# Row maxima of the first query block taken inside the projections, which load its keys block by block, last tokens first

## What is computed

```python
# layer 0, causal
q = (x @ W_q) ; lat = x @ W_dkv
lat = (lat - mean) * rsqrt(var + 1e-5) * ln_gamma + ln_beta
k = lat @ W_uk ; v = lat @ W_uv
q = apply_rope(q) ; k = apply_rope(k)
scores = einsum('bhqd,bhkd->bhqk', q, k) / sqrt(16)      # masked above the diagonal
out = einsum('bhqk,bhkd->bhqd', softmax(scores), v) @ W_o
# layer 1, not causal: Q, K, V from x by wq, wk, wv; rope on Q and K; softmax(Q K / 4) V
```

## Time and profile before

| what | value |
|---|---|
| median of 3 runs | 5580.25 us (5573.52 to 5586.86) |
| the profiled execution | 5566.02 us, its span 5564.2 us |
| mean granted clock of TensorE | 0.936 |
| busy: TensorE, VectorE, ScalarE, POOL | 91%, 85%, 67%, 4% |
| projections of layer 0, then of layer 1 | 2 to 195 us, 2345 to 2472 us |

### The profile page before, as it was taken

The page is one execution under the profiler, slowest core; times in us unless marked ns, Lnnn a source line. Parts: engine busy times, 40 slices in busy tenths (PEclk is TensorE's granted clock), DMA queues, the critical chain, the costliest instruction groups (busy, mean ns, idle before and its releaser), DMA issues. The chain is left out here.

```text
span 5564.2 us, 124831 instructions
## 1 busy us (share of the span) xinstructions
PE 5047.7 (91%) x43370; PEld 2092.7 (38%) x43370; DVE 4709.1 (85%) x5375; ACT 3734.5 (67%) x7102; POOL 218.6 (4%) x278
## 2 busy tenths in 40 slices
PE   7599999999999588767999999999999999999686
PEld 4233434433444255432333333333333333333332
DVE  3588889889888689739999999999999999999535
ACT  2068787787777311123888888888888888888331
POOL 3100000000000000030000000000000000000201
PEclk7589999999999799986999999999999999999886
DMA  4301010010010100060100001000100001000000
GB/s 125 102 18 31 14 35 15 11 41 8 11 41 11 27 11 12 17 204 12 41 8 5 5 18 31 5 5 8 38 8 8 5 5 41 8 5 5 8 0 30
DMA packets 152926, 142.93 MB, mean 26 GB/s; under 512 B 72490, under 2 KB 107242, under 8 KB 152298
## 3 DMA queue, kind: packets, MB, share of 16 engines
q1 hardware_dynamic: 152330, 134.93, 8.6%
HBM read 86.84 MB, written 46.66 MB: 24 GB/s over the span
## 5 line engine op out<-in xcount | busy, mean ns | idle before, releaser
L926 DVE TENSOR_REDUCE att_mx<-ps 128x2 f32<-128x1024 f32 (+2 forms) x3335 | 3899.7, 1193 | 284.9 <-PE ps L801 208.5
L907 ACT ACTIVATE att_probs<-ps 128x512 f32<-128x512 f32 (+3 forms) x6400 | 3388.7, 583 | 644.1 <-PE ps L843 202.0
L870 PE MATMUL ps<-att_probs,att_V 128*17 128x256 f32 (+1 forms) x25088 | 1950.0, 385 | 0.0
L843 PE MATMUL ps<-att_Q,K 50*128 50x512 f32 (+3 forms) x6400 | 1675.8, 491 | 44.6 <-ACT att_probs L907 24.8
L801 PE MATMUL ps<-K,att_Q 48*128 48x512 f32 x6670 | 1460.0, 419 | 140.2 <-DMA K<-khi_scratch 81.7
L843 PEld LDWEIGHTS ps<-att_Q,K 50*128 50x128 f32 x6400 | 649.9, 184 | 1383.1 <-ACT att_probs L907 1314.8
L870 PEld LDWEIGHTS ps<-att_probs,att_V 128*17 128x17 f32 x25088 | 426.7, 96 | 1054.5 <-issue 590.3
L801 PEld LDWEIGHTS ps<-K,att_Q 48*128 48x128 f32 x6670 | 668.2, 192 | 229.0 <-DVE att_mx L926 138.0
L887 ACT ACTIVATE att_negT<-ps 32x128 fp32r<-32x128 f32 x66 | 16.6, 252 | 231.9 <-PE ps L811 231.9
L1181 PE MATMUL ps<-wguT,mlp_xqT 128*128 128x512 f32 (+1 forms) x384 | 163.4, 577 | 0.5 <-DVE mlp_h L1284 0.2
L791 PE MATMUL ps<-att_band,att_pick 64*128 64x128 bf16 x2080 | 162.9, 224 | 0.0
(11 more groups left out here) (211 smaller groups left out, 2424.6 us busy)
## 6 DMA issues: line engine op xcount, KB each, us to landing
K<-khi_scratch SPq DMA_DIRECT2D x320, 64.0 KB, 2.3
att_Q<-qhi_scratch SPq DMA_DIRECT2D x272, 64.0 KB, 2.3
att_V<-v_scratch SPq DMA_DIRECT2D x80, 136.0 KB, 2.5
K<-klo_scratch SPq DMA_DIRECT2D x160, 64.0 KB, 2.3
v_scratch<-proj_vpad SPq DMA_DIRECT2D x16, 544.0 KB, 3.4
att_Q<-qlo_scratch SPq DMA_DIRECT2D x136, 64.0 KB, 2.3
att_Q<-att_negT SPq DMA_DIRECT2D x264, 4.0 KB
proj_x<-in_L_attn_x SPq DMA_DIRECT2D x8, 512.0 KB, 5.4
```

The lines of the kernel that those rows point to most:

```text
L843: mm = pe.matmul(ring(at)[:, lo:QB], K[rows, u // NQB, j, kt * P:(kt + 1) * P], Q[rows, slot_of(u), j, lo:QB], start=True, stop=not diagonal)
L870: mm = pe.matmul(ps[VW * h:VW * h + HV, 6, lo:(part + 1) * (QB // 2)], V[:, v // NQB, kt, HV * h:HV * (h + 1)], probs[:, (n_key[v] + kt) % ...
L907: act.activation(probs[:, (n_key[u] + kt) % PBUFS, column(h), lo:QB], ring(at)[:, lo:QB], ACT.Exp, scale=SCALE).then_inc(emptied, 1)
L926: dve.tensor_reduce(mx[:, min(u % NQB, 1), :, j, qt, c], ps[:, 2 + 2 * pair:4 + 2 * pair, 0:max_width(u, i) // 2], AX.X, ALU.max).then_inc ...
```

## The change

`project` walks over the blocks from the last tokens to the first (`block_of(j) = NB - 1 - j`), so unit 0's queries come from its first block. A new class `Lead` holds K, Q, the table of maxima `mx` and the masks over both stages. After step i's stores SP loads keys of the block before (`lead_keys(i - 1)`), and once the queries (`lead_queries`). TensorE and VectorE take the 8 items of block i-2 during block i, at fixed places (`leads`), on banks 2 and 3 alone. The items of the last two blocks stand at the end, on two pairs of banks. q and k share banks 4 and 5 now: `rows` for k waits for both q products, and for q for both k products of the block before. Ahead of attention's loop stay the gather and, in layer 1, 7 items of unit 1; SP loads the queries of unit 1, places the maxima, and loads the values. The masks are made in `project`. Tiles of `project` and `mlp_weights` are laid over `a_all` and `b_all`.

```diff
+class Lead:
+    def __init__(self, nc, ctx):
+        self.K = sbuf(nc, ctx, "K", [P, 2, PAIRS, T], F32R)
+        self.Q = sbuf(nc, ctx, "Q", [P, 4, PAIRS, QB], F32R)
+        self.mx = sbuf(nc, ctx, "mx", [P, 2, 2, PAIRS, QT, NQB])
+        self.pick = sbuf(nc, ctx, "pick", [P, 2, P], BF16)
+        self.band = sbuf(nc, ctx, "band", [P, 2, 2, P], BF16)
...
-        q_ps, k_ps = ps[:, 2:4, :], ps[:, 4:6, :]
+        q_ps = k_ps = ps[:, 4:6, :]
+        block_of = lambda j: NB - 1 - j
+        firsts = [(j, qt) for qt in range(QT) for j in range(PAIRS)]
+        ITEMS = len(firsts)
...
+                def lead_keys(i):
+                    for a in range(2):
+                        sp.wait_ge(stored["k"][a], LANDED * (i + 1))
+                    toks = slice(block_of(i) * B, (block_of(i) + 1) * B)
+                    for n, a in enumerate(K_SLOTS):
+                        for b in range(2):
+                            at = b * HALF + n * HD
+                            sp.dma_start(lead.K[at:at + HD, 0, :, toks].bitcast(F32),
...
+                                         ).then_inc(key_in[i], 16)
...
                     if i < NB:
                         store_v(i)
                         store("q", 1, i)
+                    if i == 1:
+                        lead_queries()
+                    if i >= 1:
+                        lead_keys(i - 1)
...
                 def rows(name, weight, j):
-                    if j >= 1:
-                        pe.wait_ge(prods[name], j * 2)
+                    if name == "k":
+                        pe.wait_ge(prods["q"], (j + 1) * 2)
+                    elif j >= 1:
+                        pe.wait_ge(prods["k"], j * 2)
...
+                def lead_max(i, n, pair=0, bufs=1):
+                    if n == 0:
+                        pe.wait_ge(key_in[i], 96)
...
+                    if i * ITEMS + n >= bufs:
+                        pe.wait_ge(max_taken, i * ITEMS + n + 1 - bufs)
+                    j, qt = firsts[n]
+                    c = block_of(i)
+                    max_pair(pe, ps, lead, pair, 3, 0, j, qt, c, L0 and c == NQB - 1).then_inc(max_scored, 1)
+
+                def leads(i, *which):
+                    if i >= 2:
+                        for n in which:
+                            lead_max(i - 2, n)
...
                 for i in range(NB):
+                    leads(i, 0)
                     pe.wait_ge(kept, number["x", 1, i] + 1)
...
+                        leads(i, 1)
                         rows("q", wqp[:].rearrange("p c a n -> p c (a n)"), i)
                     else:
                         rows("q", wq, i)
+                        leads(i, 1)
                         rows("k", wk, i)
-                    if i + 1 < NB:
-                        turn(i + 1)
+                    leads(i, 2)
+                    turning = turn(i + 1) if i + 1 < NB else iter(())
+                    next(turning, None)
+                    leads(i, 3)
+                    next(turning, None)
+                    if not L0:
+                        leads(i, 4)
...
+                        leads(i, 4)
+                        pe.wait_ge(prods["q"], (i + 1) * 2)
...
+                    leads(i, 5)
                     tokens_v(i)
+                    leads(i, 6, 7)
+                pe.wait_ge(prods["k"], NB * 2)
+                for i in range(NB - 2, NB):
+                    for n in range(ITEMS):
+                        lead_max(i, n, pair=(n + 1) % 2, bufs=2)
...
                 for i in range(NB):
+                    leads(i, 0)
...
+                        leads(i, 1)
                         angle("q", 0, i)
+                        leads(i, 2)
...
                         ins.then_inc(lat_normed, 1)
+                        leads(i, 3)
                         angle("q", 1, i)
                     else:
                         angle("q", 0, i)
+                        leads(i, 1)
                         angle("q", 1, i)
+                        leads(i, 2, 3)
                     if i >= 1:
                         leave("k", i - 1)
+                    leads(i, 4)
                     angle("k", 0, i)
+                    leads(i, 5)
                     angle("k", 1, i)
+                    leads(i, 6)
                     leave("q", i)
+                    leads(i, 7)
                 leave("k", NB - 1)
...
-    before_loop = [(0, i) for i in range(len(maxima(0)))] + [(1, i) for i in range(ahead[-1])]
+    before_loop = [(1, i) for i in range(ahead[-1])]
...
-                load_queries(0, 0)
-                for piece in range(NQB):
-                    load_keys(0, 0, piece)
                 load_queries(0, 1)
                 place_max(-1, 0)
+                for piece in range(NQB):
+                    load_values(0, 0, piece)
```

More of the change, by code:

```diff
@@ L147, with max_pair, project @@
 NB = NT // TB
-def project(nc, core, ps, ident, layer, x_dram, x_all, w, tables, q_parts, k_parts, v_dram, ones_to=None):
+def max_pair(pe, ps, lead, pair, slot, par, j, qt, c, diagonal):
+    wide = (qt + 1) * P if diagonal else QB
+    for b in range(2):
+        rows = slice(b * HALF, b * HALF + SROWS)
+        mm = pe.matmul(ps[:, 2 + 2 * pair + b, 0:wide], lead.Q[rows, slot, j, qt * P:(qt + 1) * P],
+                       lead.K[rows, par, j, c * QB:c * QB + wide], start=True, stop=not diagonal)
+    if diagonal:
+        for m in range(2):
+            for b in range(2):
+                rows = slice(b * HALF, (b + 1) * HALF)
+                mm = pe.matmul(ps[:, 2 + 2 * pair + b, qt * P:wide], lead.pick[rows, m], lead.band[rows, m, 0],
+                               start=False, stop=(m == 1))
+    return mm
+def project(nc, core, ps, ident, layer, x_dram, x_all, w, tables, q_parts, k_parts, v_dram, lead, spare, unused=None):
     B = TB * P
@@ L202, in project @@
         v_set = core.sem(pre + "v_set")
+        key_in = [core.sem(f"{pre}key_in_{i}") for i in range(NB)]
+        q_in = core.sem(pre + "q_in")
+        max_scored = core.sem(pre + "max_scored")
+        max_taken = core.sem(pre + "max_taken")
         if L0:
@@ L491, in leave, with lead_taken, leads @@
                                       ).then_inc(lo_made[name], 1)
+                def lead_taken(i, n, pair=0):
+                    j, qt = firsts[n]
+                    c = block_of(i)
+                    width = (qt + 1) * P if L0 and c == NQB - 1 else QB
+                    dve.wait_ge(max_scored, i * ITEMS + n + 1)
+                    dve.tensor_reduce(lead.mx[:, 0, :, j, qt, c], ps[:, 2 + 2 * pair:4 + 2 * pair, 0:width], AX.X,
+                                      ALU.max).then_inc(max_taken, 1)
+                def leads(i, *which):
+                    if i >= 2:
+                        for n in which:
+                            lead_taken(i - 2, n)
                 if L0:
@@ L788, in _, with add_band @@
             def _(pe):
-                def add_band(dst, b, kind, m):
+                def add_band(dst, b, m):
                     rows = slice(b * HALF, (b + 1) * HALF)
-                    return pe.matmul(dst, pick[rows, m], band[rows, m, kind], start=False, stop=(m == 1))
+                    return pe.matmul(dst, lead.pick[rows, m], lead.band[rows, m, 1], start=False, stop=(m == 1))
                 def take_max(i, u, at, pair):
@@ L795, in take_max @@
                     pe.wait_ge(max_taken, at + 1)
-                    diagonal = on_diagonal(u, c)
-                    wide = (qt + 1) * P if diagonal else QB
-                    bank = lambda b: ps[:, 2 + 2 * pair + b, :]
-                    for b in range(2):
-                        rows = slice(b * HALF, b * HALF + SROWS)
-                        mm = pe.matmul(bank(b)[:, 0:wide], Q[rows, slot_of(u), j, qt * P:(qt + 1) * P],
-                                       K[rows, u // NQB, j, c * QB:c * QB + wide], start=True, stop=not diagonal)
-                    if diagonal:
-                        for m in range(2):
-                            for b in range(2):
-                                mm = add_band(bank(b)[:, qt * P:wide], b, 0, m)
-                    mm.then_inc(max_scored, 1)
+                    max_pair(pe, ps, lead, pair, slot_of(u), u // NQB, j, qt, c, on_diagonal(u, c)).then_inc(max_scored, 1)
                 def turn_max(count, at):
@@ L930, in gather @@
                 def gather(count, u, taken):
-                    dve.wait_ge(max_taken, taken + 2)
+                    if taken is not None:
+                        dve.wait_ge(max_taken, taken + 2)
                     steps = Chain(dve, neg_steps, count, NEG_STEPS)
```

152 lines of the change are left out of this document (88 added, 64 removed).

## The result

The changed kernel takes 5614.66 us (median of four runs, 5613.7 to 5619.28), the kernel before on the same chip 5576.89 us (5562.71 to 5586.86). The ratio is 1.0071, its 95% interval 1.005 to 1.0091: slower by 38 us (0.7%), where 60 were forecast. The two profiled executions lie 53 us apart (spans 5617.4 and 5564.2 us).

What follows compares the result with a forecast made beforehand. It took TensorE to set the projections' pace, VectorE having gaps, with keys loading idly in the seams. Layer 0 +3 and layer 1 +57 made +60 on the median 5580.25: 5640 us, range 5562 to 5695.

Steps and rivals of the forecast that it cites:

- Third block's start: Projections: third block starts later, at 65.0 instead of 54.24 us in layer 0, 2398.3 instead of 2383.28 in layer 1.
- Blocks three to seven, layer 0: Layer 0's projections: five blocks (starts 3 to 7) take 35.0 us each, against 22.5 before.
- Blocks, layer 1: Layer 1's projections: blocks from the third on take 36.3 us each, against 14.4 before.
- The clock mixture: Projections' matmuls run between full and half clock; all full would give 5594 us, all half 5689.
- From block 7 to the first score: Seams: keys land, sixteen items 18.9 us, restart 1.2, then 15.0 of queries, placing and values.
- the 3.4 at line rate: Seam's value loads: 3.4 us if 272-byte rows ran at line rate, against about 7.2 taken.
- The seam's totals: First score against before: layer 0 310.1 against 307.1 (+3), layer 1 2651.2 against 2594.1 (+57).
- Costed at nothing: Masks moved on POOL, reversed token order, overlaid tiles, POOL's rotations and ACT's casts: no time added.
- A: Rival, projections: VectorE's and TensorE's gaps swallow the items, keys in time; 5428 us; chance 0.18, with cases towards B.
- B: Rival, projections: keys in time, rest as forecast; blocks 29.3 and 31.7 us, no late third start; 5568; chance 0.10.
- C: Rival, projections: TensorE at half clock throughout; 5689 us; chance 0.12.
- D: Rival, seams: the maxima don't leave the seam; excluded by the diff, no chance given.

Runs made afterwards that it cites:

- keys only: Changed kernel with early key loads kept, all 64 items back behind the projections, q and k on their own banks; 5509.94 us, ratio 0.9891.
- mixed: Changed kernel with layer 0 as in keys first and layer 1 as in keys only; 5489.5 us, ratio 0.9856.
- keys first: Changed kernel with SP's order altered: q's load, k's low store and six key loads ahead of the stores of q and v; 5542.56 us, ratio 0.9954.
- the SP edit: Changed kernel with q's low store and the key loads put ahead of v's store on SP; 5626.94 us, ratio 1.0088.
- the seventh item: Changed kernel with the seventh pair of a block moved ahead of v's matmuls on TensorE; 5659.18 us, ratio 1.0155.

## Why the forecast was right, and where its terms were off

The direction and the mechanism held. The forecast said that the items would leave the seam and that each block would grow by what its last transfer waits for. Point by point, on the profiled executions:

- **Third block's start.** Layer 0: 65.0 forecast, 68.66 measured (the item's pair). Layer 1, from the first turn: 46.9 forecast (2398.3 less 2351.4), 50.1 measured. Both were 3 to 4 us short. In layer 0 q's low store went out at 58.69 and not at the 55.39 of the earlier trace rows: the block before it had begun 2.6 later. That is scatter between executions rather than the change: the second block begins at 32.2 us in eight of the twelve profiled executions and at 34.8 in the other four, among them keys only, which has no item in its blocks. In layer 1 it went out 40.6 us behind the first turn where the sum had 38.5, since the first two blocks are 18.0 us apart and not 14.3 + 2.65; the rest is the first four query issues, 3.06 us where the earlier trace rows has 1.73.
- **Blocks three to seven, layer 0.** 35.0 forecast, 32.7 measured (68.66 to 232.3 in five), so 11 us of the sum were too much. The worked chain had every reduce and rotation in a row; the leftover of q came at 190.99, 24.8 us after its block's first item at 166.20, where the sum had 26.8 (28.0 less 1.2). A slip of 0.4 us is in that sum: a pair of 0.8 and k's 2.7 us behind 17.0 end at 20.5 and not at 20.1.
- **Blocks, layer 1.** 36.3 forecast, 37.5 measured, 6 us too little. The clock mixture was nearly right in its sum (q, k and v 15.6 us against 17.1) and wrong in its places: k's matmuls, which begin 10 us behind the block's head, took 3.70 us where 5.2 was put, and v's two groups took 3.78 each, 7.56, where 4.8 was put.
- **From block 7 to the first score.** 70.1 and 71.4 forecast, 68.0 and 70.4 measured. Within it the wait for queries, placing and values was 15 us and measured 13.3 (287.07 to 300.36), with the values as last wait, as forecast. From the first value load to the first score are 7.8 us where the sum had 9.6 (7.2 and 2.4 to land); the eight issues alone take 4.29, so how long the bytes took is not shown, and the trace decides neither for the 7.2 nor for the 3.4 at line rate.
- **The seam's totals.** Layer 0 +3 forecast and -7 measured; layer 1 +57 and +65. Together +60 and +58.5. The 4 and 1 us that came back elsewhere make the 53 of the two profiles. From there to the 38 between medians is the profiled executions' own scatter: before's was 11 under this comparison's median, the changed one's about 5 over it.
- **"Costed at nothing."** POOL's masks, the reversed order and the overlays: among TensorE's waits in the blocks read here POOL does not stand, and ACT stands for copies that the sum had, besides 0.3 us a block ahead of the latent's turn. The masks, the order and the overlays were not undone one by one, so that they cost nothing is not shown.
- **The rivals.** A (it hides, 152 us gained) is excluded by the blocks; mixed, at 5489.5, reaches 80 of its 152 us by another order. B (keys in time, 12 us under the kernel before) is the kernel keys first in effect, which is 27 us under it by the medians and 19 in the seams; its blocks were 27.2 and 34.1 where B had 29.3 and 31.7, so B's two errors too have opposite signs. C (half clock throughout) is excluded by the 3.70 us of k's matmuls, yet it nearly describes layer 1 in keys first, where q and k took 6.54 and 6.60. D (the maxima stay) is excluded: 16 reduces stand in the seam, not 64.

The terms that were mis-sized are layer 0's block (11 us too much over five) and layer 1's block with its third start (9 too little); they nearly cancel. That the seams' sum came out within 2 us of the forecast is luck; the waits, their causes and the order of size of each term are not.

## What to carry to other kernels

A load that is moved into an earlier stage inherits everything ahead of it in its queue's program: before the edit is made, ask for each instruction ahead of it what it waits for, and follow that up to the engine that finishes last. Here six loads of 64 KB stood behind a store nobody needed yet, and their place alone was worth 65 to 72 us. Where such a chain has two links in series, cutting one shows next to nothing (the SP edit) or a loss (the seventh item, 20 us in the seams), and only both together show what they cost, so test them together before calling either harmless. And work moved into another stage's gaps should be priced by what it does to the engine that sets the pace there: the same items cost 0.6 us each in layer 0, where the granted clock was 0.73 already, and some 2.1 in layer 1, where TensorE was busy 99 of 115 us at full clock. In one block of layer 1 in keys first the items bring 5.6 us of waits for their reduces, and q's, k's and v's matmuls take 18.7 us where they took 11.1.

## What the runs showed that was not expected

- **The clock multiplies small waits.** In layer 1 waits of 6.2 to 7.8 us for keys were followed by q's matmuls of 5.7 to 6.6 us (once 4.93), waits of 1.7 to 1.9 us, or transposes ahead of the wait, by 3.70. So taking 6 us of waiting away gave 10 a block.
- **Half clock without a wait for keys.** In keys first TensorE's waits in layer 1 are the short ones for VectorE (27.7 us in 25 waits, at most 1.9, and six of about 3.1 for q's products), and its matmuls of q and k ran near half clock all the same, with a mean of 0.74. Which of these gaps keeps it there was not tried. The Trainium skill, TensorE: Matmul & The Clock Gate, A second HAM failure mode, describes a kernel whose brief idle times between groups of matmuls, from cycling through PSUM banks, make the clock oscillate; the trace agrees with that as far as the mean of 0.74 goes.
- **The same program between the seams** took 2033 to 2063 us in the profiled executions. Cut into stretches of 300 us from the first score on, the four longest (2050 to 2063 us) each have one or two of their first five stretches at 0.90 to 0.95, the two shortest none under 0.97; but one of 2040 us has 0.95 too, so the clock is not all of it. What sets this off stays open; it is as large as several of the effects compared here, which is why lengths within the seams were read beside the medians.
